# Neighbour shifts in bf16 parts, a router bias on VectorE, maxima moved by transfers and sigmoids by tanh, in a two-layer attention and mixture-of-experts kernel

## The chip, the cores and the metric

The kernel runs on one core of one Trainium2 chip. The metric is the device time of one execution in microseconds (us), lower is better; three executions of the kernel before gave 832.26, 834.16 and 834.95. The core has five engines with instruction queues of their own, which run in order and meet only at semaphores: TensorE (PE, matrix products into PSUM), VectorE (DVE), ScalarE (ACT), GpSimd (POOL) and SyncE (SP), which here only issues transfers.

## The reference, cut to what matters

The input is 16 sequences ("batches") of 512 tokens with 256 features. Between the parts stand layer norms, which are left out here.

```python
# layer 0: causal attention with 16-wide q and k, values are x itself
scores = where(mask, einsum('bqe,bke->bqk', q, k) / 4, -10000)
x = einsum('bqk,bkv->bqv', softmax(scores), x)      # then a ternary 256x256 projection

# layer 1, attention part: one number per token from statistics of q and k
attn_base = ((num / (den + 1e-07)) ** 2)[..., 0]    # [b, 512]
h = conv1d(A[:, None, :], conv1_w)                  # 1 -> 4 channels, 3 taps along the tokens
h = relu(groupnorm(h, 2 groups) * gn_g + gn_b)
A = A + conv1d(h, conv2_w) + conv2_b                # 4 -> 1 channel, 3 taps
weights = softmax(sigmoid(A), axis=1)
ch_w = sigmoid(relu(mean(x) @ ch_w1 + ch_b1) @ ch_w2 + ch_b2)
out = (weights[..., None] * v * ch_w) @ proj_w + proj_b

# layer 1, feed-forward part: a router picks one of 8 experts for each token
logits = layernorm(x) @ router_w.T                  # the expert's gate is a softmax of these
out = shared_expert(x) + gate * expert[argmax(logits)](x)   # then residual and layer norm
```

## The kernel before

A batch is four tiles of 128 tokens. The first some 610 us work batch by batch through both attentions, the router and the shared expert, and write each token's record to DRAM at a place sorted by expert. The remaining time gathers 36 groups of up to 256 tokens by expert and runs the experts; the change touches nothing there.

**Order.** Every engine's program is written out by hand, call by call: `pe_program`, `act_program`, `dve_program`, `pool_program` and `sp_program` define small functions (a stage `name(b, i)` of batch b) and then list the calls. A loop `for g in range(2, 8)` interleaves stages of batches 2g-5 to 2g+1, so one pass advances two batches and there are six passes; a prologue and an epilogue are written out before and after. I call the part of a pass with the scores of batch 2g its even half and that with the scores of batch 2g+1 its odd half. Each stage increments the semaphore of its name, and waits name the stage and the batch.

**Scores and maxima.** TensorE computes the scores of a tile row (`score`), `max_` (L1987) reduces each to the negated row maximum, a column of `NM`. Four one-row products with an identity (`nmrow`, L567) turn the four columns into a row in `banks[0]`, and ScalarE copies it to row 96 of `Qs` (`nmr_`, L1334). `scoreT` (L578) then computes the transposed scores with the maxima subtracted by that row, `exp` follows, and `pv` (L592) multiplies with x.

**Gate.** `gate1`, `gate_r`, `gate2` give the 256 channel sums; `chw` has four VectorE steps (add bias, clip at -80, add 1, reciprocal) with `gexp` on ScalarE (Exp of -x, L1404) between the second and the third; `PS_` reads the result.

**The ODE stage.** `ode(g, k)` are 27 small VectorE steps for two batches together, on tiles of 8 to 96 columns. Steps 0 to 7 form A in `o_A`, repeated for the four channels. `nb` (L716 to L720) shifts A by one token each way with five fp32 products (within a tile by `from_prev` and `from_next`, across tiles by the `edge` matrices). Step 8 (L2207) weights the taps and step 9 sums them; `gn1` (L726) and `gn2` (L732, L733) sum over tokens for the group norm, gn2 with a second product for the epsilon; step 13 (L2221) reads the variance, GpSimd raises it to -0.5 (`gnr`, L3478), step 14 (L2225) uses it; step 19 (L2236) ends the second convolution's taps, and `nb2` (L741 to L745) shifts them with five more fp32 products. Steps 20 to 23 and `oexp` are the sigmoid, `oexp2`, step 24, `osum` and steps 25 and 26 the softmax. In the loop this stage lies in the odd half.

**Around it.** `TTl_` (L2048) subtracts the rounded part of a transposed tile of bank 3; `x2T(b, 1)` (L631) writes the next tile to the same bank and waits for `TTl_(b, 0)`. `pv(b, 2)` waits for `x1(b, 0)`.

**Router.** `logits` is 16 small bf16 products (L777) and one fp32 product from a single row, which adds the bias `RB` as a fourth part (L780). `router` has seven VectorE steps, `rank` on TensorE waits for the sixth.

Of the kernel before, what the change touches and what calls it, by code (L numbers as in the profile page):

```python
# [57 lines left out]
    "qks": NT, "chw": 4, "Ml": 1, "x3": NT, "HTl": 2, "Sl": FC, "y": NT, "r": 2, "rg": 1, "rout": 7, "acc": 2, "rank": 1, "place": 3, "hid": 1,  # L58
# [15 lines left out]
def program(nc, t, ctx):  # L74
# [14 lines left out]
    def ring(name, n, shape, dt=F32):  # L89
# [54 lines left out]
    RB = sb("RB", [1, NE])  # L144
# [53 lines left out]
    o_A = sb("o_A", [P, GB, CH, NT])  # L198
# [13 lines left out]
    epsx = sb("epsx", [P, GB * CH * NT])  # L212
# [108 lines left out]
        "bn0 bng mv0 mvg ve0 ve1 ve2 veg rs1 rs2 rsg csum bias padrow wqk bqk w0l "  # L321
# [43 lines left out]
    A_flat = o_A[:].rearrange("p b c j -> p (b c j)")  # L365
    A_one = o_A[:, :, 0, :]
    NO = 27


    def sp_program():  # L370
# [60 lines left out]

        sp.dma_start(wqk[:], first[0][1]).then_inc(s["wqk"], 16)
# [35 lines left out]
        load_x(15)  # L468
        one_e1(7)
# [65 lines left out]
    def pe_program():  # L535
# [25 lines left out]
        def nmrow(b):  # L561

            if not 0 <= b < B:
# [6 lines left out]
        def scoreT(b, k):  # L570
# [3 lines left out]
            pe.wait_ge(s["nmr"], at("nmr", b))  # L574
# [129 lines left out]
        taps = [banks[2][:, k * GW:(k + 1) * GW].rearrange("p (n j) -> p n j", j=NT) for k in range(TAPS)]  # L704
        A_tok = o_A[:].rearrange("p b c j -> p (b c) j")

        def nb(g):
            if not 0 <= g < B // GB:
                return
            pe.wait_ge(s["ode"], NO * g + 8)  # L710
# [5 lines left out]
            pe.matmul(taps[0], from_prev[:], A_tok, start=True, stop=False)  # L716
            pe.matmul(taps[0][:, :, 1:NT], edge_prev[:], A_tok[:, :, 0:NT - 1], start=False, stop=True)
            pe.matmul(taps[1], ident[:], A_tok, start=True, stop=True)
            pe.matmul(taps[2], from_next[:], A_tok, start=True, stop=False)
            pe.matmul(taps[2][:, :, 0:NT - 1], edge_next[:], A_tok[:, :, 1:NT], start=False, stop=True).then_inc(s["nb"], 1)  # L720

        def gn1(g):
            if not 0 <= g < B // GB:
                return
            pe.wait_ge(s["ode"], NO * g + 10)
            pe.matmul(banks[2][:, 0:GW], onesN[:], h_flat, start=True, stop=True).then_inc(s["gn1"], 1)  # L726

# [9 lines left out]
        def nb2(g):  # L737
            if not 0 <= g < B // GB:
                return
            pe.wait_ge(s["ode"], NO * g + 20)  # L740
            pe.matmul(out2, from_prev[:], o_t[:, 0], start=True, stop=False)  # L741
            pe.matmul(out2[:, :, 1:NT], edge_prev[:], o_t[:, 0][:, :, 0:NT - 1], start=False, stop=False)
            pe.matmul(out2, ident[:], o_t[:, 1], start=False, stop=False)
            pe.matmul(out2, from_next[:], o_t[:, 2], start=False, stop=False)
            pe.matmul(out2[:, :, 0:NT - 1], edge_next[:], o_t[:, 2][:, :, 1:NT], start=False, stop=True).then_inc(s["nb2"], 1)  # L745
# [2940 lines left out]
```

## Time and profile before

| | |
|---|---|
| median of three runs | 834.16 us (832.26 to 834.95) |
| profiled execution | 832.9 us, span of the profile 831.6 us |
| TensorE busy | 749.8 us (90%), 5485 products |
| VectorE busy | 701.7 us (84%), 2072 instructions |
| ScalarE busy | 662.1 us (80%) |
| GpSimd busy | 340.9 us (41%) |
| chain that ended last | 63% TensorE, 16% ScalarE, 5% VectorE |

The busy share of an engine is an average over the whole span. Starts of instructions in a timeline are exact enough to be subtracted; ends of products are modelled, and neighbouring products overlap, so what one product costs its engine is the step from its start to the start of the next.

### The profile page before, as it was taken

What the parts mean: (1) busy time and instruction counts of PE and PEld (TensorE: products, weight loads), DVE (VectorE), ACT (ScalarE), POOL (GpSimd) and SP (SyncE); (2) the same over time, 40 slices, a digit from 0 to 9 for tenths busy, and PEclk for the clock granted to TensorE, in tenths of its full rate; (3) what the DMA queues carried; (4) which work ended last, traced back from release to release, by engine and by line L of the source; (5) the groups of instructions that cost most, each with busy time, mean ns of one, the idle gap of its engine ahead of it and who ended that gap; (6) DMA issues with size and microseconds to landing.
All of it is one profiled execution on the core that took longest, in us unless ns stands there. A gap on an engine that the chain in (4) does not pass through costs nothing.

```text
span 831.6 us, 18563 instructions
## 1 busy us (share of the span) xinstructions
PE 749.8 (90%) x5485; PEld 597.5 (72%) x5485; DVE 701.7 (84%) x2072; ACT 662.1 (80%) x1457; POOL 340.9 (41%) x370
## 2 busy tenths in 40 slices
PE   2789999999999999999999999999675999988872
PEld 1468777787877878888787887887543777777762
DVE  4867877899889889889988988988757799999885
ACT  2456668987997987898799798796744899999994
POOL 3000020133524224243342522337635299886767
PEclk9969999999999999999999999999868999999997
DMA  7113210202222131131213220102114458765430
GB/s 258 27 54 100 76 52 26 84 26 78 71 89 96 53 102 59 55 130 39 78 65 96 90 77 33 51 27 71 58 46 140 122 164 233 211 182 163 148 119 30
DMA packets 50306, 76.50 MB, mean 92 GB/s; under 512 B 8541, under 2 KB 31007, under 8 KB 50208
## 3 DMA queue, kind: packets, MB, share of 16 engines
q1 hardware_dynamic: 39104, 48.42, 20.0%
q0 software_dynamic: 9600, 25.25, 8.4%
q10 hardware_dynamic: 1504, 1.64, 0.6%
q8 instruction: 47, 0.77, 0.4%
q14 instruction: 51, 0.42, 0.2%
HBM read 47.42 MB, written 28.91 MB: 92 GB/s over the span
## 4 chain that ended last, share of the span: by engine, by line
PE 63%; ACT 16%; issue 9%; DVE 5%; POOL 4%; ACTq 1%; DMA 0%; DVEq 0%; POOLq 0%; SPq 0%
PE bank L592 8%; ACT G_S L1904 6%; PE bank L799 6%; PE bank L812 6%; PE bank L672 4%; ACT G_y L1920 3%; PE bank L544 3%; PE bank L674 3%; PE bank L673 3%; PE bank L684 3%; PE bank L620 2%; PE bank L621 2%; ACT G_T L1880 2%; PE bank L604 2%; PE bank L767 2%
## 5 line engine op out<-in xcount | busy, mean ns | idle before, releaser
L3462 POOL TENSOR_TENSOR R<-rstd,mhalf 128x4 f32<-128x4 f32 x16 | 19.5, 1220 | 278.8 <-DVE rstd L1961 278.8
L3633 POOL DMA_INDIRECT out<-G_y,Gid x72 | 83.6, 1161 | 35.4 <-ACT G_y L1920 13.2
L1904 ACT ACTIVATE G_S<-bank,e1b,e1s 128x256 f32<-128x256 f32 (+1 forms) x188 | 95.1, 651 | 2.2 <-PE bank L1285 2.2
L1285 PE MATMUL bank<-G_T,E1T 128*128 128x256 f16 (+1 forms) x752 | 76.4, 251 | 8.0 <-issue 4.4
L592 PE MATMUL bank<-X,PT 128*128 128x257 f32 x320 | 81.0, 392 | 1.1 <-DVE X L2005 0.9
L3506 POOL DMA_INDIRECT rrec<-R,pos x64 | 67.0, 1047 | 29.2 <-issue 20.7
L3497 POOL DMA_INDIRECT hrec<-HN,pos x64 | 65.7, 1027 | 29.0 <-issue 16.0
L1297 PE MATMUL bank<-E2T,G_Sh 128*128 x288 | 65.6, 274 | 9.5 <-DVE G_Sl L3437 9.2
L1285 PEld LDWEIGHTS bank<-G_T,E1T 128*128 x752 | 59.7, 99 | 19.6 <-issue 11.6
L812 PE MATMUL bank<-E2T,Sh 128*128 128x256 f16 x256 | 60.8, 282 | 6.3 <-DVE Sl L2138 6.3
L1297 PE MATMUL bank<-E2T,G_Sl 128*128 x288 | 65.8, 275 | 0.0
L592 PEld LDWEIGHTS bank<-X,PT 128*128 128x128 f32 x320 | 58.4, 194 | 10.2 <-issue 1.6
L799 PE MATMUL bank<-HT,E1T 128*128 128x512 f16 x240 | 63.3, 394 | 0.3 <-DVE p_oh L2278 0.3
L3471 POOL TENSOR_TENSOR R<-V,mhalf 128x8 f32<-128x8 f32 x16 | 33.5, 2097 | 70.8 <-DVE V L1971 70.8
L812 PE MATMUL bank<-E2T,Sl 128*128 128x256 f16 x256 | 60.6, 282 | 0.0
L1920 ACT ACTIVATE G_y<-G_y,gnb,rstd 128x256 f32<-128x256 f32 x72 | 54.6, 762 | 7.3 <-DVE gnb L3422 7.3
L1480 ACT ACTIVATE S<-bank,e1b,e1s 128x512 f32<-128x512 f32 x64 | 49.1, 768 | 11.3 <-PE bank L799 11.1
L672 PE MATMUL bank<-WCh,TTh 128*128 128x512 f32 x128 | 56.9, 444 | 0.0
L3437 DVE SCALAR_TENSOR_TENSOR G_Sl<-G_S,sdn,G_Sh 128x1024 f16<-128x1024 f32 x36 | 46.8, 1300 | 10.9 <-ACT G_Sh L1913 10.9
L2138 DVE SCALAR_TENSOR_TENSOR Sl<-S,sdn,Sh 128x512 f16<-128x512 f32 x64 | 47.4, 743 | 6.0 <-ACT Sh L1489 6.0
L3626 POOL TENSOR_TENSOR rstd<-rstd,mhalf 128x2 f32<-128x2 f32 x36 | 45.2, 1255 | 15.4 <-DVE rstd L3416 14.9
L674 PE MATMUL bank<-WCh,TTl 128*128 128x512 f32 x128 | 51.0, 399 | 0.0
(392 smaller groups left out, 2459.2 us busy)
## 6 DMA issues: line engine op xcount, KB each, us to landing
XT<-in_xT SPq DMA_DIRECT2D x16, 512.0 KB, 3.9
X<-in_x SPq DMA_DIRECT2D x16, 512.0 KB, 5.8
G_h<-hrec SPq DMA_DIRECT2D x25, 257.0 KB, 3.6
G_r<-rrec SPq DMA_DIRECT2D x25, 257.0 KB, 3.5
e1n<-in_ew SPq DMA_DIRECT2D x8, 512.0 KB
e2n<-in_ew SPq DMA_DIRECT2D x8, 512.0 KB, 3.4
G_h<-hrec SPq DMA_DIRECT2D x22, 128.5 KB, 2.1
G_r<-rrec SPq DMA_DIRECT2D x22, 128.5 KB, 2.3
```

The lines of the kernel that those rows point to most:

```text
L592: last = pe.matmul(bk[:, 0:D + 1], PT[b % 2][:, o:o + P], X[b % 2][:, k, :], start=k == 0, stop=k == i)
L672: pe.matmul(bk[:], TTh[:, c, o], WCh[:, c, :], start=c == 0, stop=False)
L674: last = pe.matmul(bk[:], TTl[:, c, o], WCh[:, c, :], start=False, stop=c == DC - 1)
L799: last = pe.matmul(banks[(7, 6)[f % 2]][:], E1T[:, NE, c, f * P:(f + 1) * P], ht(b)[:, x, c, :], start=k == 0, stop=k == 3)
L812: last = pe.matmul(out, x[:, f, j * P:(j + 1) * P], E2T[:, NE, f, :], start=k == 0, stop=k == 2 * FC - 1)
L1285: last = pe.matmul(bk[:, o + a:o + b], E1T[:, e, c, ff * P:(ff + 1) * P], gt[:, x, c, a:b], start=k == 0, stop=k == 3)
L1297: last = pe.matmul(banks[w % 2][:, j * D:(j + 1) * D], x[w % NGB][:, f, j * P:(j + 1) * P], E2T[:, expert_of[w, j], f, :], start=k == 0, s ...
L1904: last = act.activation(G_S[w % NGS][:, ff, a:b], bk[:, o + a:o + b], ACT.Silu, bias=e1b[:, e, ff], scale=e1s[:, e, ff])
L1920: act.activation(yj, yj, ACT.Identity, bias=gnb4[w % 4][:, j:j + 1], scale=rstd[w % 4][:, j:j + 1]).then_inc(s["gn"], 1)
L3497: pool.indirect_dma_start(hrec[:], bass.IndirectOffsetOnAxis(pos[b % 2][:, j:j + 1], 0), HN[b % 2][:, j, :], None).then_inc(s[f"hrec{b % 2 ...
L3506: pool.indirect_dma_start(rrec[:], bass.IndirectOffsetOnAxis(pos[b % 2][:, j:j + 1], 0), R[b % 2][:, j, :], None).then_inc(s[f"rrec{b % 2} ...
L3633: pool.indirect_dma_start(t["out"], bass.IndirectOffsetOnAxis(Gid[w % NGI][:, j:j + 1], 0), G_y[w % NGY][:, j, :], None, bounds_check=TOK ...
```

## The change

Four edits, with new positions for some of the calls.

1. `nb` and `nb2` shift in bf16. The value is split into three bf16 parts whose sum is the fp32 value, and each of the five products becomes three, with bf16 matrices. `o_A` is no longer repeated for the channels, so a product has 8 or 6 columns. The splitting adds steps to `ode`: three after A (8 to 10), four before nb2 (23 to 26). The epsilon product of `gn2` is replaced by an addition on GpSimd. The sigmoid's VectorE steps are gone; the stage has 31 steps instead of 27. In the loop `nb` now stands one call later (behind `up(.., 2)`), `nb2` behind `x2T(2g, 1)`.
2. `RB` holds the bias in all rows and is added by a new step `router(b, 1)` on VectorE; L780 is gone. `router` has eight steps, `rank` waits for the seventh.
3. From batch 4 the maxima reach row 96 of `Qs` by four transfers per batch on the SP queue, one per column, each waiting for its `max_`; `nmrow` and `nmr_` remain for batches 0 to 3. `scoreT` waits for all four transfers.
4. Both sigmoids are computed as 0.5 + 0.5 tanh(x/2). `chw` has two steps instead of four; in the ODE stage tanh is followed directly by exp of half of it, as the constant cancels in the softmax.

```diff
-            pe.matmul(taps[0], from_prev[:], A_tok, start=True, stop=False)
-            pe.matmul(taps[0][:, :, 1:NT], edge_prev[:], A_tok[:, :, 0:NT - 1], start=False, stop=True)
-            ...
+            for k in range(3):
+                pe.matmul(taps[0], from_prev[:], o_Ap[:, k], start=k == 0, stop=False)
+            for k in range(3):
+                pe.matmul(taps[0][:, :, 1:NT], edge_prev[:], o_Ap[:, k, :, 0:NT - 1], start=False, stop=k == 2)
+            ...
-            pe.matmul(banks[2][:, 0:GW], onesN[:], epsx[:], start=True, stop=False)
-            pe.matmul(banks[2][:, 0:GW], onesN[:], sq_flat, start=False, stop=True).then_inc(s["gn2"], 1)
+            pe.matmul(banks[2][:, 0:GW], onesN[:], sq_flat, start=True, stop=True).then_inc(s["gn2"], 1)
```

```diff
+            elif k == 8:
+                ins = dve.tensor_tensor(o_d[:, 0], o_A[:], o_Ap[:, 0], ALU.subtract)
+            elif k == 9:
+                ins = dve.tensor_copy(o_Ap[:, 1], o_d[:, 0])
+            elif k == 10:
+                ins = dve.tensor_tensor(o_Ap[:, 2], o_d[:, 0], o_Ap[:, 1], ALU.subtract)
...
+            elif k == 23:
+                ins = dve.tensor_copy(o_tp[:, 0], o_t[:])
+            elif k == 24:
+                ins = dve.tensor_tensor(o_d[:], o_t[:], o_tp[:, 0], ALU.subtract)
+            elif k == 25:
+                ins = dve.tensor_copy(o_tp[:, 1], o_d[:])
+            elif k == 26:
+                ins = dve.tensor_tensor(o_tp[:, 2], o_d[:], o_tp[:, 1], ALU.subtract)
```

```diff
+            pool.tensor_scalar(o_rs[:], o_rs[:], 1e-5, None, ALU.add).then_inc(s["gnv"], 1)
+            pool.wait_ge(s["gnv"], g + 1)
             pool.tensor_tensor(o_rs[:], o_rs[:], mhalf[:, 0:2 * GB], ALU.pow).then_inc(s["gnr"], 1)
```

```diff
+        def maxima(b):
+            if not NROW <= b < B:
+                return
+            ...
+                for j in range(NT):
+                    sp.wait_ge(s["max"], at("max", b, j))
+                    sp.dma_start(Qs[96:97, j * P:(j + 1) * P].bitcast(F32), NM[b % 2][:, j:j + 1].bitcast(F32)).then_inc(s["nmd"], 16)
...
-            out = banks[6][:, 0:NT * W3].rearrange("p (j k e) -> p j k e", j=NT, k=4)[:, :, 3, :]
-            last = pe.matmul(out, ones[0:1, :], RB[0:1, None, :].to_broadcast([1, NT, NE]), start=True, stop=True)
...
+                ins = dve.tensor_tensor(r_lg[:], r_lg[:], RB[:, None, :].to_broadcast([P, NT, NE]), ALU.add)
```

```diff
-            act.activation(CHW[:], CHW[:], ACT.Exp, scale=-1.0).then_inc(s["gexp"], 1)
+            act.activation(CHW[:], CHW[:], ACT.Tanh, scale=0.5).then_inc(s["gexp"], 1)
...
-            act.activation(o_e[:], o_e[:], ACT.Exp, scale=-1.0).then_inc(s["oexp"], 1)
+            act.activation(o_e[:], o_e[:], ACT.Tanh, scale=0.5).then_inc(s["oexp"], 1)
...
-            act.activation(o_e[:], o_e[:], ACT.Exp).then_inc(s["oexp2"], 1)
+            act.activation(o_e[:], o_e[:], ACT.Exp, scale=0.5).then_inc(s["oexp2"], 1)
```

The calls in TensorE's list, odd half of a pass:

```diff
             fuse(2 * g - 1)
+            up(2 * g - 3, 2)
             nb(g - 1)
-            nmrow(2 * g + 1)
-            up(2 * g - 3, 2)
             up(2 * g - 3, 3)
             gn1(g - 1)
...
             pv(2 * g + 1, 1)
-            nb2(g - 1)
...
             x2T(2 * g, 1)
+            nb2(g - 1)
             pv(2 * g + 1, 2)
```

In VectorE's list `ode(g-1, 8)` to `(g-1, 10)` stand right behind `max_(2g+1, 3)` and before `Sl_(2g-3, 0)`, with `ve1(2g)` among them; `ode(g-1, 23)` to `(g-1, 26)` stand behind `TTl_(2g, 0)` and before `x1(2g+1, 0)`. On SP, `maxima(2g-1)` stands behind `load_x(2g)` and `maxima(2g)` behind `load_xT(2g+1)`.

## Rows read from the trace of the kernel before

**Rows 1.** Busy time in one pass: us, each engine, PE clock, DMA share, GB/s.

```profile
332.00:402.00 70.00, 70.00 (x493) 56.24 (x491) 62.65 (x192) 59.96 (x137) 25.22 (x24) 1.00 0.23 77
```

**Rows 2.** TensorE's timeline, even half: start us, busy us, line, out<-in, count.

```profile
344.36 0.40 PE L578 MATMUL bank<-Qs,Ks 128*128 128x512 f32 x1
...
344.97 0.55 PE L777 MATMUL bank<-RW,HT 128*128 128x24 bf16 x16
345.45 0.40 PE L780 MATMUL bank<-RB,ones 1*128 1x32 f32 x2
345.78 1.04 PE L799 MATMUL bank<-HT,E1T 128*128 128x512 f16 x4
```

**Rows 3.** TensorE's timeline, odd half of the same pass.

```profile
381.11 0.30 PE L716 MATMUL bank<-o_A,from_prev 128*128 128x32 f32 x2
...
382.14 0.40 PE L567 MATMUL bank<-identr,NM 128*1 128x128 f32 x4
382.38 1.90 PE L799 MATMUL bank<-HT,E1T 128*128 128x512 f16 x8
384.12 0.30 PE L726 MATMUL bank<-o_h,onesN 128*128 128x32 f32 x2
...
386.14 0.30 PE L732 MATMUL bank<-epsx,onesN 128*128 128x32 f32 x2
...
390.61 0.37 PE L741 MATMUL bank<-o_t,from_prev 128*128 128x8 f32 x2
...
391.73 0.63 PE L631 MATMUL bank<-ident,X 128*128 128x128 f32 x4
392.20 3.21 PE L592 MATMUL bank<-X,PT 128*128 128x257 f32 x14
```

**Rows 4.** VectorE's timeline, even half: the last maximum of batch 2g.

```profile
340.82 0.68 DVE L1987 TENSOR_REDUCE NM<-bank 128x1 fp32r<-128x512 f32 x1
```

**Rows 5.** VectorE's timeline, odd half: the ODE stage's steps that bind.

```profile
380.43 0.68 DVE L1987 TENSOR_REDUCE NM<-bank 128x1 fp32r<-128x512 f32 x1
...
382.41 0.26 DVE L2207 TENSOR_TENSOR o_T<-bank,W1x 128x96 f32<-128x96 f32 x1 [0.56 <-PE bank L720]
...
386.77 0.19 DVE L2221 TENSOR_REDUCE o_rs<-bank 128x4 f32<-128x32 f32 x1
...
388.62 0.18 DVE L2225 TENSOR_TENSOR o_h<-o_h,o_rs 128x32 f32<-128x32 f32 x1
...
390.21 0.33 DVE L2236 TENSOR_REDUCE o_t<-o_T 128x24 f32<-128x96 f32 x1
390.44 0.69 DVE L2048 TENSOR_TENSOR TTl<-bank,TTh 128x512 fp32r<-128x512 f32 x1
```

**Rows 6.** GpSimd: the power in its timeline, an addition-like step in its groups by line.

```profile
387.06 1.41 POOL L3478 TENSOR_TENSOR o_rs<-o_rs,mhalf 128x4 f32<-128x4 f32 x1 [2.82 <-DVE o_rs L2221]
...
L3534 POOL TENSOR_SCALAR desc<-iota_f 128x8 f32<-128x8 f32 x1 | 0.2, 196 | 0.1
```

**Rows 7.** VectorE's timeline: two small steps that depend on each other, nothing between them.

```profile
608.09 0.19 DVE L2115 TENSOR_REDUCE r_mx<-r_lg 128x4 f32<-128x32 f32 x1
608.32 0.19 DVE L2118 TENSOR_TENSOR r_eq<-r_lg,r_mx 128x32 f32<-128x32 f32 x1
```

**Rows 8.** DMA issues: out<-in, queue, count, KB each, median us from issue to landing.

```profile
hrec<-hpad SPq DMA_DIRECT2D x10, 128.5 KB, 4.4
...
bqk<-in_bqk ACTq DMA_DIRECT2D x1, 0.5 KB, 2.2
cb<-in_cb SPq DMA_DIRECT2D x1, 0.2 KB, 3.1
```

**Rows 9.** ScalarE: table loads at the gate's exponential by line, and the ODE stage's exponential.

```profile
L1404 ACT ACT_TABLE_LOAD x7 | 9.0, 1283 | 0.1
...
393.68 0.21 ACT L1437 ACTIVATE o_e<-o_e 128x8 f32<-128x8 f32 x1
```

**Rows 10.** Chain of waits in the epilogue, the bias product of batch 14.

```profile
600.07 0.58 PE bank L780 x2
```

More of the change, by code:

```diff
@@ L430, in pad_rows @@
                 sp.dma_start(rrec[r, :], rpad0[:]).then_inc(s["zero"], 16)
+        def maxima(b):
+            if not NROW <= b < B:
+                return
+            with nc.allow_non_contiguous_dma(reason="a column of each tile into one row"):
+                for j in range(NT):
+                    sp.wait_ge(s["max"], at("max", b, j))
+                    sp.dma_start(Qs[96:97, j * P:(j + 1) * P].bitcast(F32), NM[b % 2][:, j:j + 1].bitcast(F32)).then_inc(s["nmd"], 16)
         sp.dma_start(wqk[:], first[0][1]).then_inc(s["wqk"], 16)
@@ L561, in nmrow @@
         def nmrow(b):
-            if not 0 <= b < B:
+            if not 0 <= b < NROW:
                 return
@@ L739, in nb2 @@
                 return
[L740 to L745, printed above, removed]
+            pe.wait_ge(s["ode"], NO * g + 27)
+            for k in range(3):
+                pe.matmul(out2, from_prev[:], o_tp[:, k, 0], start=k == 0, stop=False)
+            for k in range(3):
+                pe.matmul(out2[:, :, 1:NT], edge_prev[:], o_tp[:, k, 0, :, 0:NT - 1], start=False, stop=False)
+            for k in range(3):
+                pe.matmul(out2, identb[:], o_tp[:, k, 1], start=False, stop=False)
+            for k in range(3):
+                pe.matmul(out2, from_next[:], o_tp[:, k, 2], start=False, stop=False)
+            for k in range(3):
+                last = pe.matmul(out2[:, :, 0:NT - 1], edge_next[:], o_tp[:, k, 2, :, 1:NT], start=False, stop=k == 2)
+            last.then_inc(s["nb2"], 1)
         def osum(g):
@@ L1330, in nmr_ @@
         def nmr_(b):
-            if not 0 <= b < B:
+            if not 0 <= b < NROW:
                 return
@@ L2763, in dve_program @@
         x2(2, 1)
-        for i in range(8, 11):
+        for i in range(11, 14):
             ode(0, i)
         ve1(2)
-        for i in range(11, 14):
+        for i in range(14, 17):
             ode(0, i)
@@ L2873, in dve_program @@
             router(2 * g - 4, 0)
+            router(2 * g - 4, 1)
             if g == 0:
                 rest(7)
-            for i in range(1, 4):
+            for i in range(2, 5):
                 router(2 * g - 4, i)
@@ L3171, in dve_program @@
         x3(13, 0)
-        chw(14, 2)
-        router(11, 6)
+        router(11, 7)
         one0(7, 0)
@@ L3198, in dve_program @@
         x2(15, 0)
-        for i in range(4):
+        for i in range(5):
             router(12, i)
         rg(11)
-        router(12, 4)
         router(12, 5)
+        router(12, 6)
         one0(7, 1)
@@ L3231, in dve_program @@
         TTl_(15, 1)
-        router(12, 6)
+        router(12, 7)
         rg(12)
@@ L3254, in dve_program @@
         router(13, 0)
+        router(13, 1)
         ode(7, 0)
@@ L3257, in dve_program @@
         ode(7, 1)
-        router(13, 1)
+        router(13, 2)
         ode(7, 2)
         ode(7, 3)
-        router(13, 2)
+        router(13, 3)
         ode(7, 4)
         ode(7, 5)
-        router(13, 3)
+        router(13, 4)
         ode(7, 6)
-        router(13, 4)
+        router(13, 5)
         ode(7, 7)
-        router(13, 5)
+        ode(7, 8)
+        ode(7, 9)
+        ode(7, 10)
+        router(13, 6)
         r(12, 1)
-        ode(7, 8)
+        ode(7, 11)
         place(13, 0)
         one0(7, 4)
-        ode(7, 9)
+        ode(7, 12)
         x2p(15)
-        for i in range(10, 13):
+        for i in range(13, 16):
             ode(7, i)
         Sl_(13, 0)
-        ode(7, 13)
+        ode(7, 16)
         one1(7, 3)
@@ L3281, in dve_program @@
         Sl_(13, 1)
-        for i in range(14, 17):
+        for i in range(17, 20):
             ode(7, i)
         place(13, 1)
-        for i in range(17, 20):
+        for i in range(20, 27):
             ode(7, i)
@@ L3288, in dve_program @@
         place(13, 2)
-        for i in range(20, 24):
-            ode(7, i)
+        ode(7, 27)
         acc(13)
-        ode(7, 24)
+        ode(7, 28)
         Sl_(13, 3)
-        ode(7, 25)
-        ode(7, 26)
+        ode(7, 29)
+        ode(7, 30)
         for i in range(4):
             x3(14, i)
-        router(13, 6)
+        router(13, 7)
         y(13, 0)
@@ L3315, in dve_program @@
         router(14, 1)
-        for i in range(2, 6):
+        router(14, 2)
+        for i in range(3, 7):
             router(14, i)
         place(14, 0)
-        router(14, 6)
+        router(14, 7)
         HTl_(15, 0)
@@ L3322, in dve_program @@
         acc(14)
-        for i in range(6):
+        for i in range(7):
             router(15, i)
@@ L3357, in dve_program @@
         sort(9)
-        router(15, 6)
+        router(15, 7)
         y(15, 0)
```

274 lines of the change are left out of this document (135 added, 139 removed), and 2 rows, old and new, of the table names.

## The prediction

> **What bounds the kernel now.** I read the busy times by stretch first. In a pass of the loop TensorE is busy all 70 us at the full granted clock, VectorE 62.65 and ScalarE 59.96 [rows 1]. The six passes issue the same calls, so the pass of 332 to 402 us stands for them. Then I read the engines' timelines side by side, because a full TensorE says that its products follow one another, not that nothing else is late: at several places another engine delivers just in time. The clearest is nb2. VectorE ends its input (L2236) at 390.21 + 0.33 = 390.54, and nb2 starts at 390.61 [rows 3, 5]. Whatever TensorE saves ahead of that place within the same half pass becomes a wait there, unless VectorE's chain comes earlier too. So each edit has two prices, the issue time on TensorE and the shift of the chain that ends at nb2 and x2T.
>
> All starts below are those of this pass. Sums are made against the profiled execution, 832.9 us; the median of the runs shown is 834.16, and the same difference is applied to it.
>
> **TensorE, even half.** L780 starts at 345.45 and the next product at 345.78: 0.33 us go with it [rows 2]. nmrow costs 382.38 - 382.14 = 0.24 in the odd half [rows 3]; I take the same here. Its other cost, the ScalarE copy, lay beside other work. What is late next is scoreT: it must wait for the transfer of the last maximum. That maximum ends at 340.82 + 0.68 = 341.50 [rows 4]; scoreT began at 344.36 [rows 2], and would be reached at 344.12. Allowing 0.1 for SP to start, a landing time up to 2.5 us costs nothing. No row of before shows a transfer of 128 single elements from 128 partitions into one row. The nearest is bqk, the same shape turned round (128 elements of 4 bytes), 2.2; then cb 3.1, and 4.4 for 128 rows into DRAM [rows 8]. From below it can be no gain, since the wait for the maximum remains. I take 2.2, because its elements have the same size and number: no stall. At 3.1 it is 0.6, at 4.4 it is 1.9. Queued behind the waiting scoreT are logits, up and everything else of TensorE, so such a stall counts in full. On SP the transfers stand where the next load waits for a later proj anyway, so they delay no load. Even half: -0.57.
>
> The Trainium skill, DMA: Bandwidth & Descriptors, section Anatomy of one DMA — SWDGE (gpsimd) path, gives about 2.0 us of setup and completion whatever the size, which would also mean no stall. The same page, section Rules for kernel authors, says that a non-contiguous last dimension becomes one descriptor per element; by that rule the four transfers are 512 descriptors, which speaks against the edit, and no row shows what they take.
>
> **TensorE, odd half.** L780 gives 0.33 again. nb costs 382.14 - 381.11 = 1.03 now. The new one has 15 bf16 products of 6 or 8 columns; 16 bf16 products of 24 columns step by (345.45 - 344.97) / 16 = 0.03 [rows 2], so it costs 0.45. nb2 goes from 391.73 - 390.61 = 1.12 to the same 0.45 [rows 3]. Counted alone, these, the 0.24 of nmrow and about 0.14 for the missing product of gn2 would give 1.6 us. The chain decides how much of it survives:
> - nb's input needs three more dependent VectorE steps behind the maximum at 380.43. Two dependent small steps stand 0.23 apart [rows 7], so they end near 381.8. nb now stands behind one up, half of the 1.74 that L799 took for two (384.12 - 382.38) [rows 3]: it starts at 381.11 + 0.87 = 381.98 without waiting, ends its issue at 382.43, and VectorE's step 11 (L2207) starts at about 382.6 instead of 382.41 [rows 5].
> - From there to the read of the variance VectorE's list is unchanged and was 386.77 - 382.41 = 4.36 long, with only short waits; so that read comes at 386.96. TensorE, which arrives early at gn1 and gn2, waits for it. The gains of nb, nmrow and gn2 are used up here. It also means 0.4 us of cover for the transfers: with 2.2 the last lands at 381.2 + 0.1 + 2.2 = 383.5, and scoreT is reached only at 383.9.
> - GpSimd does one more instruction. 0.2 us for the addition (L3534) and 0.15 for its semaphore, against 1.41 for the power [rows 6]. Bounds: 0.2, and 1.4 if a small addition cost what a power costs. I take 0.35, by the nearer kind of operation. Step 17 then starts at 386.96 + (388.62 - 386.77) + 0.35 = 389.16, against 388.62. Queued behind it on VectorE are the rest of the stage and TTl.
> - TTl(2g, 0) follows 390.44 - 388.62 = 1.82 later, at 390.98, and ends at 391.67 [rows 5]. x2T(2g, 1) starts at 391.7, where it started at 391.73, and takes 0.47. The four splitting steps run behind TTl: 390.98 + 0.6 + 4 x 0.23 = 392.5. nb2 starts there and ends its issue at 392.95. pv(2g+1, 2) started at 392.20 [rows 3]. Loss 0.75.
>
> So the odd half gives -0.33 + 0.75 = +0.42, and a pass -0.57 + 0.42 = -0.15. The bounds of the loss of 0.75 are -1.6 (all issue time counts, the chain has cover that I do not see) and +1.8 (the GpSimd addition at 1.4).
>
> **ScalarE.** Tanh at 393.68 [rows 9] needs no VectorE step before exp; that shortens the softmax's tail by some 0.5 us, but osum's place behind pv hides it. The gate's Exp comes right after Silu in odd batches and brings a table load, 7 of 1.28 us [rows 9], and each brings Silu's own back. If Tanh is found in both tables, up to 14 loads or 18 us of ScalarE go; if in neither, the ODE stage gains two. ScalarE has 10 us of slack per pass and no wait of TensorE in the loop ends on these, so I count 0. The Trainium skill, ScalarE: Activation LUTs, section Table sets: the hidden batching unit, lists tanh beside exp; it says nothing of silu's set. By it no load is added in the ODE stage.
>
> **VectorE.** 7 more steps in two batches and 2 more for the router, less 3 of the sigmoid and 4 of the gates, at about 0.1 us of issue: under 1 us per pass in 7 us of slack.
>
> **Prologue and epilogue.** The first ODE stage loses like the others, but without the gain of batches' logits: +0.3 (from 0 to 0.75). Batch 12's L780 lies on TensorE's path, -0.33. In batches 14 and 15 the bias product stands on the chain itself with 0.58 [rows 10] (two such rows, 0.58 and 0.56); the router's new step takes 0.23 back in batch 14 and is hidden behind up in 15: -0.35 and -0.56. The last ODE stage is a bare chain: three splitting steps (0.7, half covered by fuse), the addition (0.35) and four more (0.92), against two shorter shifts (1.25) and 0.5 less for the sigmoid, +0.15. Together -0.8.
>
> **The sum.** 6 x (-0.15) - 0.8 = -1.7. 832.9 becomes 831.2; the median 834.16 becomes 832.5.
>
> **Rivals.**
> (a) The chain has more cover. If GpSimd's addition hides and TTl comes 0.5 earlier, the loss of 0.75 is 0.1: 6 x 0.65 = 3.9 less, 828.6. If no wait follows at all, a pass gives -0.57 - 0.33 - 1.6 = -2.5, six give -15, with 2 more outside: 817. For it: TensorE never waits in the loop, and VectorE has short idle gaps there. Against it: the 0.07 us between L2236 and nb2.
> (b) The transfers land late, so it is slower. Place: scoreT of the even half. Price: everything beyond 2.5 us, and beyond 3.0 in the odd half. At 3.6 us it is 1.1 + 0.6 per pass, +10: 842.5. It decides for slower from about 3.2 us on. For it: the 3.1 and 4.4 of rows 8, both queued behind other transfers of their queue; against it the 2.2 and a DMA share of only 0.23 [rows 1].
> (c) The tables do not help: Tanh shares none with Exp. Then two loads of 1.28 join the ODE stage in front of osum, which has about 1.4 of cover, and two the gate: about +1.2 per pass, 840.
> (d) The stage's chain is longer than I made it (GpSimd at 1.4, splitting steps at 0.3): +1.3 per pass, 840.
>
> **Chances.** Forecast as worked out 0.45; (a) 0.28, of it 0.06 for 817; (b) 0.13; (c) 0.04; (d) 0.10. What a measurement of this kernel can tell from no change is about 0.3%, 2.5 us: below 831.7 or above 836.7. The forecast lies 0.8 us from the lower bound, so a third of it, 0.14, counts as faster: faster 0.41, same 0.35, slower 0.24. The range goes from 826, which leaves out the far part of (a), to 840.5, which leaves out half of (b).
>
> **What would show it.** Right: the product that opens the pv group behind nb2 starts later than before relative to fuse, with waits of TensorE at gn1, gn2, x2T (about 1.1 us, for TTl) and nb2; no wait of scoreT on the transfer; transfers of 0.5 KB with 2.0 to 2.5 us to landing; L1404 without table loads or with the same seven, and the time indifferent to which; passes shorter by some 0.15 us. Wrong: a scoreT that waits on NM or Qs for over 0.3 us, a pass shorter by more than 0.8 us, or a table load at L1437.

## The result, and the profile after

The change made the kernel slower. Four executions gave 844.26, 845.46, 848.11 and 850.35 us, four of the kernel before 832.26 to 834.95: the ratio is 1.0159, with a 95% interval of 1.0127 to 1.0192. The profiled execution took 845.46 us (span 844.1 us) against 832.9 us (span 831.6 us) before, 12.5 us more. The forecast was 832.5, from 826.0 to 840.5.

The pass that starts at 332 before starts some 5 us later now. First its busy times, by stretch; the columns are those of [rows 1].

```profile
332.00:402.00 70.00, 67.61 (x475) 53.01 (x474) 61.69 (x190) 55.43 (x130) 25.77 (x24) 0.98 0.24 76
```

TensorE, which was busy for all 70 us, now has 2.4 us of gaps, and the mean of its granted clock is 0.98 instead of 1.00. The waits of TensorE in the loop (200 to 560 us; total, times, longest) name the places. The same view of the kernel before is empty.

```profile
PE bank L648 <- DVE TTl L2069: 9.2, 5, 1.9
PE bank L748 <- DVE o_h L2235: 1.9, 5, 0.4
```

To subtract positions, each half is measured from its `fuse`. Before, TensorE's timeline:

```profile
340.92 0.81 PE L684 MATMUL bank<-PS,wvT 128*128 128x256 f32 x3
...
379.33 1.08 PE L684 MATMUL bank<-PS,wvT 128*128 128x256 f32 x4
```

and after, where the lines answer to [rows 2, 3]:

```profile
346.20 0.60 PE L701 MATMUL bank<-PS,wvT 128*128 128x256 f32 x2
...
349.38 0.40 PE L595 MATMUL bank<-Qs,Ks 128*128 128x512 f32 x1
...
350.39 1.02 PE L824 MATMUL bank<-HT,E1T 128*128 128x512 f16 x4
...
383.48 0.65 PE L701 MATMUL bank<-PS,wvT 128*128 128x256 f32 x2
...
386.12 0.22 PE L733 MATMUL bank<-o_Ap,from_prev 128*128 128x8 bf16 x3
...
386.50 1.02 PE L824 MATMUL bank<-HT,E1T 128*128 128x512 f16 x4
387.90 0.41 PE L748 MATMUL bank<-o_h,onesN 128*128 128x32 f32 x2 [0.37 <-DVE o_h L2235]
...
396.68 0.66 PE L648 MATMUL bank<-ident,X 128*128 128x128 f32 x4 [1.85 <-DVE TTl L2069]
397.46 0.24 PE L763 MATMUL bank<-o_tp,from_prev 128*128 128x8 bf16 x3
...
397.95 4.66 PE L609 MATMUL bank<-X,PT 128*128 128x257 f32 x14
402.45 0.28 PE L778 MATMUL bank<-o_s,ones 128*128 128x2 f32 x2
```

| step, us from its fuse | before | after | difference |
|---|---|---|---|
| scoreT, even half | 344.36 - 340.92 = 3.44 | 3.18 | -0.26 |
| up behind logits, even half | 345.78 - 340.92 = 4.86 | 4.19 | -0.67 |
| next fuse (odd half) | 379.33 - 340.92 = 38.41 | 37.28 | -1.13 |
| x2T(2g, 1) | 391.73 - 379.33 = 12.40 | 13.20 | +0.80 |
| pv(2g+1, 2) | 392.20 - 379.33 = 12.87 | 14.47 | +1.60 |
| osum | 395.28 - 379.33 = 15.95 | 18.97 | +3.02 |

So the even half and the stretch up to the odd fuse keep 1.13 us, somewhat more than forecast: 0.26 from nmrow and 0.41 and 0.46 from the two bias products. The odd half gives 1.60 away up to the pv group and then 1.42 more inside it: the same 14 products take 402.45 - 397.95 = 4.50 us instead of 3.08. A pass (odd fuse to odd fuse) is 383.48 - 311.82 = 71.66 us against 379.33 - 309.59 = 69.74.

The first loss starts on VectorE and GpSimd. Their timelines, answering to [rows 5, 6]:

```profile
390.97 0.18 DVE L2246 TENSOR_REDUCE o_rs<-bank 128x4 f32<-128x32 f32 x1
391.07 0.68 DVE L2414 TENSOR_SCALAR ev<-e1n 128x1024 f16<-128x1024 f32 x1
391.67 1.22 DVE L2063 TENSOR_TENSOR X<-X,pb_row 128x1024 f32<-128x1024 f32 x1
394.21 0.19 DVE L2250 TENSOR_TENSOR o_h<-o_h,o_rs 128x32 f32<-128x32 f32 x1 [1.32 <-POOL o_rs L3508]
...
395.95 0.68 DVE L2069 TENSOR_TENSOR TTl<-bank,TTh 128x512 fp32r<-128x512 f32 x1
```

```profile
391.25 1.73 POOL L3506 TENSOR_SCALAR o_rs<-o_rs 128x4 f32<-128x4 f32 x1 [3.43 <-DVE o_rs L2246]
393.06 1.04 POOL L3508 TENSOR_TENSOR o_rs<-o_rs,mhalf 128x4 f32<-128x4 f32 x1
```

The addition of 1e-5 to four columns takes 1.73 us. From the read of the variance to the step that uses its root it is 394.21 - 390.97 = 3.24 us, where [rows 5] give 388.62 - 386.77 = 1.85: 1.39 more. The addition ends at 391.25 + 1.73 = 392.98, the long VectorE addition beside it (L2063, two SBUF operands) at 391.67 + 1.22 = 392.89.

The second loss is a clock. Granted clock by stretch (last columns: PEclk, DMA share, GB/s), over the pv group of the first pass and then of the pass above:

```profile
184.40:187.50 3.10, 3.10 (x15) 2.69 (x15) 3.10 (x10) 1.66 (x7) 0.14 (x1) 1.00 0.12 42
397.95:399.00 1.05, 1.05 (x6) 0.86 (x4) 1.05 (x4) 1.02 (x6) 0.14 (x1) 0.50 0.35 125
399.00:400.00 1.00, 1.00 (x4) 0.82 (x3) 0.66 (x2) 0.15 (x1) 0.00 (x0) 0.50 0.00 0
400.00:401.00 1.00, 1.00 (x5) 0.79 (x4) 0.10 (x2) 0.00 (x0) 0.00 (x0) 0.62 0.00 0
```

0.50 is the lower level, 1.2 GHz. TensorE had waited 1.85 us just before. But so it had in the first pass, where the clock stayed at 1.00 and the group took 3.11 us:

```profile
183.12 0.66 PE L648 MATMUL bank<-ident,X 128*128 128x128 f32 x4 [1.85 <-DVE TTl L2069]
184.39 3.28 PE L609 MATMUL bank<-X,PT 128*128 128x257 f32 x14
187.50 0.28 PE L778 MATMUL bank<-o_s,ones 128*128 128x2 f32 x2
```

That first pass is only 0.55 us longer than before (240.19 - 169.90 against 239.85 - 170.11), the others 1.9. The same wait costs 1.4 us more or nothing more, depending on whether the clock falls.

Last, ScalarE's table loads (Silu's before; then Silu's, L1503, and the attention exp's, L1351, after) and the transfers:

```profile
L1480 ACT ACT_TABLE_LOAD x15 | 19.2, 1283 | 0.3
```

```profile
L1503 ACT ACT_TABLE_LOAD x8 | 10.3, 1283 | 0.1
L1351 ACT ACT_TABLE_LOAD x6 | 7.7, 1283 | 0.1
```

```profile
Qs<-NM SPq DMA_DIRECT2D x48, 0.5 KB, 1.9
```

The loads at the gate [rows 9] are gone, and Silu's (L1503) are 8 instead of 15: 14 loads less, none at the ODE stage's tanh. A transfer of the maxima lands 1.9 us after its issue, and TensorE waits for none in the loop.

### The profile page after: what moved, and what is told of

Same layout as the page of the kernel before. It is cut to its first block and busy times, and to the rows that moved or that the text cites. A ratio compares the mean times of both kernels' runs of the same rounds, so it can differ in the third digit from the quotient of the medians.

```text
span 844.1 us, 18577 instructions
## 1 busy us (share of the span) xinstructions
PE 742.6 (88%) x5469; PEld 583.3 (69%) x5469; DVE 707.2 (84%) x2096; ACT 637.4 (76%) x1431; POOL 346.5 (41%) x378
## 5 line engine op out<-in xcount | busy, mean ns | idle before, releaser
L3490 POOL TENSOR_TENSOR R<-rstd,mhalf 128x4 f32<-128x4 f32 x16 | 16.9, 1054 | 273.7 <-DVE rstd L1982 273.7
L3663 POOL DMA_INDIRECT out<-G_y,Gid x72 | 83.4, 1158 | 37.0 <-ACT G_y L1941 14.2
L1925 ACT ACTIVATE G_S<-bank,e1b,e1s 128x256 f32<-128x256 f32 (+1 forms) x188 | 90.0, 602 | 3.1 <-PE bank L1308 2.7
L609 PE MATMUL bank<-X,PT 128*128 128x257 f32 x320 | 89.2, 422 | 0.7 <-DVE X L2026 0.5
L609 PEld LDWEIGHTS bank<-X,PT 128*128 128x128 f32 x320 | 63.7, 212 | 12.0 <-issue 1.3
L824 PE MATMUL bank<-HT,E1T 128*128 128x512 f16 x240 | 65.5, 401 | 0.3 <-DVE p_oh L2304 0.3
L1503 ACT ACTIVATE S<-bank,e1b,e1s 128x512 f32<-128x512 f32 x64 | 49.0, 767 | 13.5 <-PE bank L824 13.4
L1941 ACT ACTIVATE G_y<-G_y,gnb,rstd 128x256 f32<-128x256 f32 x72 | 49.7, 694 | 7.3 <-DVE gnb L3450 7.3
L690 PE MATMUL bank<-WCl,TTh 128*128 128x512 f32 x128 | 51.1, 399 | 0.0
```

The source lines that it names most:

```text
L609: last = pe.matmul(bk[:, 0:D + 1], PT[b % 2][:, o:o + P], X[b % 2][:, k, :], start=k == 0, stop=k == i)
L690: pe.matmul(bk[:], TTh[:, c, o], WCl[:, c, :], start=False, stop=False)
L824: last = pe.matmul(banks[(7, 6)[f % 2]][:], E1T[:, NE, c, f * P:(f + 1) * P], ht(b)[:, x, c, :], start=k == 0, stop=k == 3)
L1925: last = act.activation(G_S[w % NGS][:, ff, a:b], bk[:, o + a:o + b], ACT.Silu, bias=e1b[:, e, ff], scale=e1s[:, e, ff])
L1941: act.activation(yj, yj, ACT.Identity, bias=gnb4[w % 4][:, j:j + 1], scale=rstd[w % 4][:, j:j + 1]).then_inc(s["gn"], 1)
L3663: pool.indirect_dma_start(t["out"], bass.IndirectOffsetOnAxis(Gid[w % NGI][:, j:j + 1], 0), G_y[w % NGY][:, j, :], None, bounds_check=TOK ...
```

## The experiments

My theory after reading the trace, T: the GpSimd addition is slow because of what VectorE runs beside it; it delays TTl and x2T, and the wait that follows lets TensorE's clock fall. Rivals: the splitting steps and nb2's new place are the cause (S); only the delay counts, and the clock falls for another reason (D); the GpSimd instruction is slow by itself (W).

Four chips were used, each with the kernel before beside the experiments. `e1_eps_product`, `e2_filler`, `e4_x2p_moved` and `b1_addition` ran on the first of them; `r_before`, `r_after`, `e6_two_parts` and `e5_nb2_late` on the second; `e2b_filler`, `e8_x1_first` and `e9_three_parts` on the third; `e10_score_first` on the fourth. The chips differ: the median of the kernel before was 846.5, 832.9, 847.2 and 850.0 us on them. So only ratios to the kernel before and positions within a pass are compared. The ratios are those on record, with their 95% intervals; they differ from the quotient of the two medians by up to 0.0024.

### The addition undone, the wait filled, the neighbour moved, the addition alone

`e1_eps_product`, the changed kernel with

```diff
-            pool.tensor_scalar(o_rs[:], o_rs[:], 1e-5, None, ALU.add).then_inc(s["gnv"], 1)
-            pool.wait_ge(s["gnv"], g + 1)
+            pe.matmul(banks[2][:, 0:GW], onesN[:], epsx[:], start=True, stop=False)
```

> The changed kernel with one thing undone: the epsilon comes by gn2's product again and GpSimd only raises to the power. Theory T: the addition costs 1.36 us on the chain to TTl, and the wait at x2T that follows lowers TensorE's granted clock, so that the pv group costs 1.42 us more. Then the wait at x2T falls from 1.85 to some 0.5 us, the clock stays at 1.00, a pass loses 2.8 us, and the time is 829 to 831, faster than the kernel before. Rival S (the splitting steps and the new place of nb2 are the cause): the pass loses under 0.5 us and the time stays above 843. Rival D (only the delay counts and the clock's fall has another cause): a pass loses 1.4 us, the time is 838.

Measured: 0.9983 (0.9960 to 1.0005) of the kernel before, against 1.0159 and 1.0137 of the whole change. Its TensorE timeline (fuse at 379.55):

```profile
391.40 0.66 PE L649 MATMUL bank<-ident,X 128*128 128x128 f32 x4 [0.27 <-DVE TTl L2071]
...
392.63 3.51 PE L610 MATMUL bank<-X,PT 128*128 128x257 f32 x14
395.98 0.28 PE L780 MATMUL bank<-o_s,ones 128*128 128x2 f32 x2
```

The wait is 0.27 instead of 1.85, the group starts 13.08 from fuse (before 12.87) and takes 3.35, with the clock at 1.00. T holds for these steps. The time of 829 to 831 us can't be read on this chip, but it would be a fall of 1.9 to 2.1% from the changed kernel, and the ratio fell by 1.5 to 1.8% only: the kernel is level with the one before and not faster. The group takes 0.27 us more than before although the clock is at 1.00, for a reason that stays open. S is out as the main cause.

`e2_filler` and, on another chip, the same kernel again as `e2b_filler`:

```diff
+            pe.wait_ge(s["ode"], NO * g + 17)
+            for _ in range(16):
+                pe.matmul(banks[2][:, 256:512], W0T[:, 0, 0:P], W0T[:, 0, :], start=True, stop=True)
             x2T(2 * g, 1)
```

> The changed kernel with 16 more products of 256 columns (their result is never read) in front of x2T(2g, 1) of each pass, where TensorE waits 1.85 us for TTl; the wait itself stays. It tells the clock from the delay. Theory T: TensorE is busy in the stretch, the granted clock stays at 1.00 over the pv group, the 14 products take 3.1 instead of 4.5 us, a pass loses 1.4 us, and the time is 838 (837 to 840). Rival D (the pv group is late for its data, or the clock falls for a reason outside this wait): no gain, 846 to 848, and if the fillers outlast the wait, up to 852.

> The same kernel as e2_filler once more, since that run fell on a chip on which every kernel showed a further wait in the even half. On a chip without that wait it can be set against the changed kernel (1.0137, pass 71.97 us, wait 1.85, pv group up to osum 4.8 us). Theory T: the granted clock stays at 1.00 over the pv group, the group falls to some 3.4 us, a pass to 70.6, the ratio is 1.003 to 1.008. Rival D (the group is late for its data): group above 4.3 us, ratio 1.013 or more.

Measured: 1.0075 (1.0049 to 1.0102) and 1.0064 (1.0034 to 1.0095). TensorE in `e2b_filler` (fuse at 387.96), and its clock over the group:

```profile
398.96 2.26 PE L777 MATMUL bank<-W0T 128*128 128x256 f32 x16
401.17 0.66 PE L648 MATMUL bank<-ident,X 128*128 128x128 f32 x4
402.44 3.45 PE L609 MATMUL bank<-X,PT 128*128 128x257 f32 x14
405.73 0.28 PE L783 MATMUL bank<-o_s,ones 128*128 128x2 f32 x2
```

```profile
402.44:405.73 3.29, 3.29 (x16) 2.65 (x15) 3.16 (x10) 1.68 (x7) 0.14 (x1) 1.00 0.11 40
```

x2T starts 13.21 from fuse, exactly as in the changed kernel, so the delay is untouched; yet the group takes 3.29 instead of 4.50 us. Work that nobody needs makes the kernel faster than the changed one by 0.6 to 1.0%, by the ratios. The 838 us expected of the first run can't be read on its chip (852.32, with the kernel before at 846.46), and the pass of 70.6 us expected of the second was missed: its passes take 71.58 to 72.79 us. They hold a further wait of 0.71 to 0.79 us at hT (a transposition in the next even half, which waits for VectorE's R) that the changed kernel does not have on its chips, and twice a wait for a transfer of the maxima. The runs speak against D, but they don't rule it out: both fell on chips of the slower kind, where no trace of the unfilled kernel exists, so it isn't shown that the clock would have fallen there without the fillers. A comparison on one chip follows with `e5_nb2_late`.

`e4_x2p_moved`:

```diff
             one0(g - 1, 4)
-            x2p(2 * g - 1)
...
             TTl_(2 * g, 1)
+            x2p(2 * g - 1)
```

> The changed kernel with x2p(2g-1), VectorE's 1.22 us addition of two SBUF operands that runs beside the epsilon's addition on GpSimd, moved behind TTl(2g, 1). Theory V (GpSimd is slowed by VectorE's long SBUF instructions): the addition of 128x4 falls from 1.73 to 0.6 to 0.9 us (the conversion L2414 still stands beside its start), VectorE's step 17 comes 0.8 to 1.1 us earlier, and with it the clock holds: a pass loses 1.0 to 2.5 us, 832 to 841. Theory W (a first instruction on GpSimd takes 1.7 us by itself after a wait): 1.73 stays, the time is 846 to 848.

Measured: 1.0047 (1.0024 to 1.0071). GpSimd's timeline:

```profile
389.88 0.59 POOL L3506 TENSOR_SCALAR o_rs<-o_rs 128x4 f32<-128x4 f32 x1 [3.42 <-DVE o_rs L2246]
390.55 1.04 POOL L3508 TENSOR_TENSOR o_rs<-o_rs,mhalf 128x4 f32<-128x4 f32 x1
```

The addition falls from 1.73 to 0.59, and the shortest of the eight, in the last ODE stage, takes 0.24. Same instruction, same operands, another neighbour: V holds, W is out. The 0.59 ends at 390.47, the VectorE conversion beside it (L2414, one SBUF operand, 389.69 + 0.68) at 390.37, so this one held it too; beside the 0.24 VectorE ran a subtraction with one of its operands in PSUM. The step that waits comes 391.69 - 389.59 = 2.10 after the variance, 0.25 more than before the change. The Trainium skill, GPSIMD Engine Reference, section Specifications, says that GpSimd shares its SBUF interfaces with VectorE and contends with VectorE instructions that have two SBUF inputs or run in a two-port mode. For the two inputs the trace agrees (1.73 against 0.59); whether L2414 runs in such a mode no trace here shows. In exchange VectorE's list is longer behind TTl, and osum now waits 0.58 us for it.

`b1_addition`, the kernel before with the addition in place of the epsilon product:

> The kernel before with one part of the change: gn2's epsilon product is gone and GpSimd adds the epsilon ahead of the power. Theory T: the addition takes 1.7 us in the loop, step 17 (here step 14) comes 1.3 us later, x2T waits some 1.3 us, a pass gains that and, if the clock falls, 1.4 more: 841 to 850, so most of the whole change's loss. Rival S: the addition hides or costs 0.35 us as forecast, 834 to 836.

Measured: 1.0139 (1.0098 to 1.018). pv(2g+1, 2) starts 399.18 - 384.94 = 14.24 from fuse, 1.37 later than before (1.26 to 1.30 in the other passes), behind a wait of 1.2 to 1.4 us at nb2 and not at x2T as expected; the addition takes 1.73 us, the clock stays at 1.00 and the group takes 3.07. So the addition alone costs some 8 us in six passes. The medians differ by 9.8 us (856.21 against 846.46), the ratio stands for 11.8, and the four executions lie between 850 and 861 us; these 2 to 4 us more are not explained.

### Both kernels again, two parts alone, nb2 later

`r_before` and `r_after` are the two kernels unchanged.

> The kernel before, unchanged, for a trace from the chip of the experiments, where its median is 846 us and not 834. All experiments so far show a wait of 0.75 us of TensorE at hT (for VectorE's R) in the even half of a pass there, which neither trace from the first chip has. If it belongs to the chip, this trace shows it too and the pass is some 70.7 to 71 us instead of 69.75; if it belongs to the edits, this trace has no wait in the loop.

> The changed kernel, unchanged, on the chip of the experiments. Theory T (addition under VectorE's long instruction, then the clock): 1.012 to 1.019 of the kernel before, addition 1.73 us, x2T waits 1.85 us, and the granted clock falls to 0.5 over the pv group as on the first chip. Rival C (the clock's fall belongs to the first chip): the clock stays at 1.00 in the loop, and the ratio is 1.005 to 1.010.

Measured: `r_before` shows no wait in the loop and a pass of 69.73. This chip is like the one of the first traces, so nothing follows on the extra wait of some 0.75 us at hT. It is in every trace from the three slower chips (in `b1_addition` in three of five passes), and so is a wait of 2.6 to 4.1 us for the input of the last ODE stage's nb, which is at most 0.9 us in the traces from the two faster chips. That both belong to the slower chips is likely, but no trace of the kernel before from one of them exists; the cause stays open. `r_after`: 1.0137 (1.0096 to 1.0178), with the same 1.85 us wait in every pass and a clock over the pv group of 1.00 in the first two passes (70.28 and 70.29 us long), while it falls to 0.50 in the others (71.97). C is out, and again equal waits have two prices.

`e6_two_parts`, the kernel before with the router's bias on VectorE and the maxima by transfers:

```diff
+                dve.wait_ge(s["rb"], b + 1)
+                ins = dve.tensor_tensor(r_lg[:], r_lg[:], RB[:, None, :].to_broadcast([P, NT, NE]), ALU.add)
...
-            pe.wait_ge(s["nmr"], at("nmr", b))
+            if b < NROW:
+                pe.wait_ge(s["nmr"], at("nmr", b))
+            else:
+                pe.wait_ge(s["nmd"], 16 * NT * (b - NROW + 1))
```

> The kernel before with two of the four edits: the router's bias on VectorE and the maxima by transfers from the fifth batch; the ODE stage, its shifts and both sigmoids as before. Theory T: these are the parts that TensorE can keep: per pass 0.41 + 0.40 (bias product) + 0.26 (one-row products, even half; in the odd half the ODE chain takes the same back), so 6 x 1.07 = 6.4 and some 1.2 us outside, ratio 0.990 to 0.993. Rival (the transfers or the new router step cost elsewhere): ratio 0.996 or more.

Measured: medians 827.21 against 832.87 us, ratio 0.9919 (0.9887 to 0.9950). One whole pass of it, by stretch:

```profile
306.20:374.80 68.60, 68.60 (x479) 55.09 (x478) 62.63 (x194) 58.80 (x134) 25.07 (x23) 1.00 0.25 78
```

A pass is 374.76 - 306.19 = 68.57 us, 1.16 less than in `r_before`, with TensorE busy throughout. The stretch from the even to the odd fuse gives 1.12 of it (38.38 to 37.26), the whole of the two bias products and the even half's nmrow; the odd half's nmrow, 0.24 of TensorE's time, brings 0.04 only, as expected of the half in which VectorE's chain is just in time. This version beats both kernels.

`e5_nb2_late`: epsilon as in `e1_eps_product`, and

```diff
             x2T(2 * g, 1)
-            nb2(g - 1)
             pv(2 * g + 1, 2)
+            nb2(g - 1)
```

> The changed kernel with the epsilon by product again (as in e1_eps_product) and nb2 one call later, behind pv(2g+1, 2) instead of ahead of it, so that TensorE works while VectorE splits the taps. In e1_eps_product pv(2g+1, 2) starts 0.75 us after nb2 could be reached. Theory T: TensorE keeps 0.3 to 0.6 us per pass more, against e1_eps_product 2 to 3.5 us in all, ratio 0.994 to 0.996. Rival: the softmax's tail (nb2, VectorE, tanh, exp, osum) is then late and osum waits for it, ratio 0.998 to 1.003.

Measured: 1.0056 (1.0030 to 1.0082), a miss: slower, and for neither reason I gave. Two rows of TensorE:

```profile
393.55 1.54 PE L610 MATMUL bank<-X,PT 128*128 128x257 f32 x6 [0.58 <-DVE X L2028]
396.32 1.98 PE L610 MATMUL bank<-X,PT 128*128 128x257 f32 x8 [0.87 <-DVE X L2028]
```

pv waits for x1, which stands behind the four splitting steps on VectorE's list. nb2's wait had hidden that. For the clock this run is the comparison on one chip: `r_after` on the same chip waits 1.85 us at x2T and its clock falls in four of six passes; here the waits are 0.2 to 0.3 us at x2T and 0.58 to 0.87 at pv, and the clock stays at 1.00 through the whole loop.

### VectorE's order mended, tanh added, gn1 behind scoreT

`e8_x1_first`, `e5_nb2_late` with

```diff
             TTl_(2 * g, 0)
+            x1(2 * g + 1, 0)
+            rinv(2 * g + 1, 1)
             ode(g - 1, 23)
             ...
             ode(g - 1, 26)
-            x1(2 * g + 1, 0)
-            rinv(2 * g + 1, 1)
+            x1(2 * g + 1, 1)
             Sl_(2 * g - 3, 2)
             ode(g - 1, 27)
-            x1(2 * g + 1, 1)
```

> e5_nb2_late with VectorE's list mended: x1(2g+1, 0) stands right behind TTl(2g, 0) again and x1(2g+1, 1) ahead of Sl, so that the four splitting steps no longer stand before x1. In e5_nb2_late pv waited 0.58 and 0.87 us per pass for x1. Theory (the splitting steps on VectorE's list, and not nb2's place, hold TensorE up): both waits go, a pass falls from 70.3 to 68.9 us, ratio 0.992 to 0.996, level with e6_two_parts, as the bf16 shifts take no longer and no less than the chain allows. Rival: the wait moves to osum or TTl(2g, 1), ratio 1.000 or more.

Measured: 0.9935 (0.9910 to 0.9961). Both waits are gone, those at gn1 (0.37) and x2T (0.27) remain; pv(2g+1, 2) starts 392.78 - 380.44 = 12.34 from fuse and osum 16.13. With every idea of the change kept except GpSimd's addition, and four calls moved (nb2, two x1, one rinv), the change is a gain. The pass of 68.9 us expected was missed: it is 69.96 to 70.06 us, with 0.70 to 0.81 of that in the wait at hT. In `e6_two_parts` osum starts 15.82 from fuse: the bf16 shifts add nothing to the gain.

`e9_three_parts` is `e6_two_parts` with both sigmoids by tanh.

> e6_two_parts with both sigmoids by tanh as in the change (14 table loads, three VectorE steps of the stage and two of each gate less); shifts and epsilon as in the kernel before. Forecast of the prediction: ScalarE and these steps are hidden, so within 0.002 of e6_two_parts' 0.9919. Rival: the table loads stand in front of someone's wait after all, ratio 0.988 or less.

Measured: 0.9942 (0.9918 to 0.9965). osum starts 15.92 from fuse (15.82 without tanh). The tanh brings no gain here. The ratio lies 0.0023 above that of `e6_two_parts`, where at most 0.002 was expected, but the intervals overlap and the chips differ, so no loss is shown either.

`e10_score_first`, `e8_x1_first` with scoreT(2g+1, 0) ahead of gn1:

> e8_x1_first with scoreT(2g+1, 0), 0.46 us of TensorE's work, ahead of gn1 instead of behind it. In e8_x1_first TensorE waits 0.37 us at gn1 for VectorE's o_h and 0.27 us at x2T for TTl in each pass. Theory (what the bf16 shifts save on TensorE is lost in waits for VectorE's chain, and comes back if other work stands in them): the wait at gn1 goes, gn1 is at most 0.1 us later, a pass loses 0.2 to 0.3 us, ratio 0.0015 to 0.003 below that of e8_x1_first, 0.9905 to 0.992. Rival: scoreT then waits for the transfer of the last maximum, or the wait at x2T grows by as much: no gain, 0.993 to 0.996.

Measured: 0.9924 (0.9896 to 0.9953), which cannot be told from 0.9935 and lies between what the theory and the rival expected. gn1 starts 4.42 from fuse in both, so scoreT fits into the wait and the wait at gn1 is gone; but among the waits in the loop are now

```profile
PE bank L716 <- DVE Ml L2099: 1.4, 5, 0.3
PE bank L649 <- DVE TTl L2071: 1.2, 5, 0.3
```

(L716 is the first of the products behind gn1), and osum stands at 16.14, as before the move. VectorE's chain sets this half, and 0.46 us of TensorE's work moved into its waits changes nothing.

## Why the prediction was wrong, point by point

- **Bias product (L780).** Forecast -0.33 twice a pass. Right; 0.41 and some 0.45 measured.
- **nmrow and the transfers.** Forecast -0.24 and a landing of 2.2 us, no stall below 2.5. Right: -0.26, 1.9 us. Rival (b) did not occur. In `e2_filler` scoreT did wait for a transfer once, for 1.17 us, and in `e2b_filler` twice, for up to 0.9 us, so the cover is thin. One figure of rival (b) doesn't fit its own working: with scoreT reached at 383.9 and the issue at 381.3 the odd half covers a landing of 2.6 us, not 3.0.
- **nb and nb2.** Forecast 0.45 us each; 0.38 and 0.49 measured. That their gain is used up by waits for VectorE was right as a mechanism: the wait at gn1 is 0.37, and `e10_score_first` shows that TensorE's time does not count there. Of the four places where waits were forecast (gn1, gn2, x2T, nb2) only gn1 and x2T show one.
- **The odd half without the addition.** Of the 0.75 loss I gave the addition 0.35, so 0.40 for the rest; `e1_eps_product` measured 13.08 - 12.87 = 0.21, and 0.27 more inside the group.
- **The GpSimd addition.** This step failed. I took 0.35 with an upper bound of 1.4; it cost 1.39. "A small instruction is short" holds beside some VectorE instructions (0.24 beside one with an operand in PSUM; 0.59 beside one with one SBUF input), but VectorE's timeline of the kernel before had the row that mattered, right where the addition had to go (after 386.96), and I priced the instruction without its neighbour. Rival (d) had the price (1.4) and 0.10 of the chance, but its 840 is still 7 us short of the measured median. With the addition at 1.4 my own bound for the loss up to the pv group held (+1.8; measured 1.60). The row:

```profile
387.48 1.22 DVE L2042 TENSOR_TENSOR X<-X,pb_row 128x1024 f32<-128x1024 f32 x1
```

- **The clock.** This step failed too: a term that I left at nothing without a reason. The forecast wait of 1.1 us at x2T was seen as lost time only. With 1.85 us the clock fell in four of the five passes from odd fuse to odd fuse and gave 1.4 us more each, which neither the sum nor a rival held. In `b1_addition` waits up to 1.4 us left it at 1.00 (on a slower chip), in `e5_nb2_late` 0.58 and 0.87 did too (on the chip of `r_after`). What decides it at 1.85 us, where it falls in some passes and not in others, is open.
- **Tanh.** Forecast: table loads go or stay, no matter. Right, 14 went and `e9_three_parts` gained nothing. Rival (c) did not occur.
- **Prologue and epilogue.** Forecast -0.8. The router of batches 14 and 15 gained 0.31 and 0.50 (from L804 at 612.10 to VectorE's L2304 at 615.05, before 599.47 to 602.73; likewise 618.90 to 621.80 and 606.57 to 609.97), as forecast. The first ODE stage lost more: osum stands 0.65 later from its fuse, and the first even fuse of the loop comes 0.9 later, where +0.3 (at most 0.75) was forecast. For the last ODE stage +0.15 was forecast; the parts that the prediction lists for it give 1.62 - 1.75 = -0.13. From fuse(15) to the logits of batch 14 it is 612.10 - 586.65 = 25.45 us against 599.47 - 576.35 = 23.12, so +2.3. But this is not the chain. Behind gn2, which starts only 0.32 later than before, the same products of TensorE take longer; before and after:

```profile
582.30 1.89 PE L799 MATMUL bank<-HT,E1T 128*128 128x512 f16 x8
583.84 0.47 PE L698 MATMUL bank<-Mh,TTh 128*128 128x256 f32 x1
```

```profile
592.90 3.60 PE L824 MATMUL bank<-HT,E1T 128*128 128x512 f16 x8
595.94 0.78 PE L715 MATMUL bank<-Mh,TTh 128*128 128x256 f32 x1
```

The eight take 3.04 instead of 1.54 us and the twelve behind them 2.87 instead of 1.78: 2.6 us. The granted clock was 0.52 from 592 to 599 us there, and 1.00 from 582 to 589 before. The other pair of traces has it the other way round: in `r_before` the clock is 0.50 from 582 to 588 us, and the same stretch takes 26.56 us against 24.58 in `r_after`. So the clock falls here in the kernel before as well, in one execution and not in another, and the +2.3 is the luck of the two profiled executions; what the last ODE stage lost by the change is not known to better than this.

The sum in measured terms, from fuse to fuse: up to the first odd fuse of the loop -0.2 (+0.9 and -1.1), a pass with the clock at 1.00 +0.55, four at 1.9 +7.5, +3.0 from the last odd fuse of the loop to fuse(14) (with the sixth pv group and its clock), -0.6 up to fuse(15), and +2.2 from there to the end: 12.5. The +0.55 against the forecast -0.15 is the addition (1.39 - 0.35 = 1.04 more), less what the other steps gave beyond their forecast; the clock is 1.4 of each 1.9. Between the forecast -1.7 and the measured +12.5 lie 14.2 us: the addition is 6 x 1.04 = 6.2 of them, the clock over five pv groups 5 x 1.42 = 7.1, the clock in the epilogue 2.6, and the remaining steps gave some 1.7 more than forecast. By this sum the median without the fallen clock would have been some 837 us, slower than before but inside the range.

## What to carry to other kernels

Before a small instruction is put on GpSimd, look at what VectorE runs at that moment: an instruction with two long SBUF operands held it to its end here, and one with a single one for 0.6 us. When a change adds a wait of TensorE where it had been busy throughout, price a second loss, the products behind it at half the clock, and look at several passes and executions, for it may come in some only. Work taken off TensorE paid in full where no other engine delivered just in time (1.12 us a pass in `e6_two_parts`); where one did, it paid next to nothing.

## What the runs showed of the hardware that I had not expected

- GpSimd's addition of 128x4 took 0.24, 0.59 or 1.73 us, by what VectorE did beside it; the two longer ones ended 0.1 us after the VectorE instruction beside them.
- After a wait of 1.85 us the granted clock was 0.50 over the next three microseconds in most passes and 1.00 in the first (in `r_after` the first two), with the same instructions. With sixteen unused products in the wait it was 1.00 in both runs, on other chips.
- An issue of 0.5 KB from 128 partitions into one row took 0.47 us of SyncE's queue and landed after 1.9 us (median of 48; 3.2 at most).
- Tanh needed no table load after Silu (at the gate) and none before Exp (in the ODE stage).
- The same kernel took 833 or 847 to 850 us, by the chip.
